# Depthwise stage of a four-layer kernel: weights and image cells loaded into partitions 8 to 119 only

## What is computed

```
A_f, B_f, gA_f, gB_f = FFTs of four 7x7 depthwise kernels
gate_A = sigmoid(ifft(gA_f * x_f));  gate_B = sigmoid(ifft(gB_f * x_f))
a_t = ifft(A_f) * gate_A;            b_t = ifft(B_f * x_f) * gate_B
log_z      = -softplus(-a_t);        log_coeffs = -softplus(a_t)
log_values = log_z + log(softplus(b_t) + 1e-6)
h_final    = exp(last of 8 steps of a log-space scan over (log_coeffs, log_values))
return h_final @ W_out + b_out
```

## Time and profile before

| | |
|---|---|
| median of 3 runs | 5486.84 us (5483.71 to 5490.64) |
| the profiled execution, device time | 5499.24 us |
| its span in the trace | 5497.5 us |
| depthwise stage, from its first to its last convolution | 4539 to 5318 us of the span |
| busy, of the whole span | PE 86%, PEld 63%, DVE 64%, ACT 54%, POOL 37% |
| weights of the depthwise stage | 256 DMAs of 512 KB, 8.1 us from issue to landing |
| windows of the depthwise stage | 128 DMAs of 528 KB, 6.1 us from issue to landing |

### The profile page before, as it was taken

The page is one execution under the profiler, slowest core; times in us unless marked ns, Lnnn a source line. Parts: engine busy times, 40 slices in busy tenths (PEclk is TensorE's granted clock), DMA queues, the critical chain, the costliest instruction groups (busy, mean ns, idle before and its releaser), DMA issues. The chain is left out here.

```text
span 5497.5 us, 111057 instructions
## 1 busy us (share of the span) xinstructions
PE 4738.3 (86%) x37534; PEld 3483.8 (63%) x37534; DVE 3512.8 (64%) x10149; ACT 2975.6 (54%) x6431; POOL 2060.1 (37%) x1516
## 2 busy tenths in 40 slices
PE   6999999999999997469999899974666569999982
PEld 5777777777777775146776677721222348988882
DVE  6778888888888786125666566612899513555554
ACT  1888888888888881123333333332555423555552
POOL 1666666666666660022332233301556300222221
PEclk8999999999999999699999999997999759999995
DMA  7222222222222229742221222255888539999982
GB/s 275 71 71 71 70 71 71 71 71 71 71 71 71 71 60 314 291 139 71 68 68 59 91 67 69 66 183 169 246 272 275 180 123 345 328 325 330 333 260 57
DMA packets 844717, 822.69 MB, mean 150 GB/s; under 512 B 65224, under 2 KB 705665, under 8 KB 835329
## 3 DMA queue, kind: packets, MB, share of 16 engines
q1 hardware_dynamic: 834386, 796.65, 46.5%
q10 hardware_dynamic: 6720, 10.76, 0.6%
q0 software_dynamic: 3072, 8.39, 0.4%
HBM read 607.88 MB, written 207.68 MB: 148 GB/s over the span
## 5 line engine op out<-in xcount | busy, mean ns | idle before, releaser
L299 POOL TENSOR_TENSOR at_bias<-at_tri,at_mask 128x1024 f32<-128x1024 f32 x512 | 1205.1, 2377 | 751.2 <-DVE at_neg_max L460 740.2
L409 ACT ACTIVATE at_probs<-at_neg_s,at_neg_max 128x256 f32<-128x256 f32 x2048 | 894.8, 502 | 0.1
L460 DVE CUSTOM_DVE_ANT_0 at_neg_s<-at_p_s,at_bias 128x256 f32<-128x256 f32 x2048 | 744.1, 420 | 47.1 <-PE at_p_s L333 47.1
L344 PE MATMUL at_p_t<-all_ident,at_probs 128*128 128x128 f32 x4096 | 628.6, 276 | 0.3 <-ACT at_probs_t L401 0.2
L1721 PE MATMUL dw_p_conv<-dw_xw,dw_wts 128*128 128x128 f32 x4096 | 512.9, 278 | 114.9 <-DMA dw_wts<-patch_w 58.5
L344 PEld LDWEIGHTS at_p_t<-all_ident,at_probs 128*128 128x128 f32 x4096 | 484.3, 141 | 136.8 <-issue 85.1
L1721 PEld LDWEIGHTS dw_p_conv<-dw_xw,dw_wts 128*128 128x128 f32 x4096 | 484.5, 192 | 131.6 <-issue 129.5
L921 ACT ACTIVATE ml_h<-ml_p,l_b 128x512 f32<-128x512 f32 x384 | 263.9, 687 | 556.3 <-PE ml_p L880 556.3
L1822 POOL TENSOR_TENSOR dw_xr<-dw_xr,all_b_plain 128x512 f32<-128x512 f32 x128 | 188.1, 1469 | 880.2 <-DMA dw_xr<-x3t 880.2
L468 DVE COPY at_probs_t<-at_p_t 128x512 f32<-128x512 f32 x512 | 352.6, 689 | 205.0 <-PE at_p_t L344 205.0
L889 PE MATMUL ml_p<-l_w1s,ml_h 128*128 128x128 f32 x4096 | 478.4, 275 | 0.8 <-issue 0.8
(11 more groups left out here) (210 smaller groups left out, 9353.4 us busy)
## 6 DMA issues: line engine op xcount, KB each, us to landing
dw_wts<-patch_w SPq DMA_DIRECT2D x256, 512.0 KB, 8.1
dw_xw<-planes SPq DMA_DIRECT2D x128, 528.0 KB, 6.1
sp_xs<-x SPq DMA_DIRECT2D x128, 512.0 KB, 9.9
planes<-pw_plane SPq DMA_DIRECT2D x128, 264.0 KB, 4.5
in_xs<-in_x_dram SPq DMA_DIRECT2D x32, 1024.0 KB, 7.7
at_xs<-in_x_dram SPq DMA_DIRECT2D x256, 128.0 KB, 2.4
at_kvs<-in_L_conv_kv_x_dram SPq DMA_DIRECT2D x256, 128.0 KB, 2.5
at_mask<-in_L_conv_mask_bias_dram SPq DMA_DIRECT2D x256, 128.0 KB, 3.3
```

The lines of the kernel that those rows point to most:

```text
L299: pool.tensor_tensor(bias[:, n % 2, part], tri[:, part], mask[:, n % 4].unsqueeze(1).broadcast_to((128, 4, COLS)), ALU.add).then_inc(maske ...
L344: mm = pe.transpose(p_t[h % 2][:, kh, qh * 128:(qh + 1) * 128], probs[:, h, qh, kh * 128:(kh + 1) * 128], ident[:, :])
L409: e = act.activation(probs[:, h, qh, :], neg_s[:, n % 2, h, qh, :], ACT.Exp, bias=neg_max[:, n % 2, i:i + 1], scale=-1.0)
L460: t = dve.tensor_tensor_reduce(neg_s[:, n % 2, h, qh, :], p_s[h][:, qh, :], bias[:, n % 2, i, :], -1.0, 3.0e38, ALU.add, ALU.min, neg_max[ ...
```

## The change

In the depthwise stage the first filling of each buffer (window loads 0 to 2, weight loads 0 to 3) stays as it is. Every later window load and weight load covers only partitions 8 to 119, 112 of the 128, and reads only those rows from HBM. Partitions 0 to 7 and 120 to 127 keep what the first filling put there: finite image values, and in the weights the zeros of the unused band rows. The number of instructions, their order, the waits and the semaphore counts are as before on every engine; the matmuls still read all 128 partitions.

```diff
-        def windows(b, c):
-
-            at = b * BLOCK_PY * PATCH * PATCH * cell + c * WIDE
-            return bass.AP(planes.tensor, at, [[cell, 128], [PATCH * PATCH * cell, BLOCK_PY], [1, run]])
+        used = slice(PATCH, 128 - PATCH)
+
+        def windows(b, c, first, count):
+
+            at = b * BLOCK_PY * PATCH * PATCH * cell + c * WIDE + first * cell
+            return bass.AP(planes.tensor, at, [[cell, count], [PATCH * PATCH * cell, BLOCK_PY], [1, run]])
...
-                sp.dma_start(flat[:, k % 3], windows(b, c)).then_inc(x_loaded[k % 3], 16)
+                rows = slice(0, 128) if k < 3 else used
+                sp.dma_start(flat[rows, k % 3], windows(b, c, rows.start, rows.stop - rows.start)).then_inc(x_loaded[k % 3], 16)
...
-                sp.dma_start(wts[:, g % 4], patch_w[g % groups]).then_inc(w_loaded[g % 4], 16)
+                rows = slice(0, 128) if g < 4 else used
+                sp.dma_start(wts[rows, g % 4], patch_w[g % groups, rows]).then_inc(w_loaded[g % 4], 16)
```

## The result

| | |
|---|---|
| before | 5488.74 us, median of 4 (5483.71 to 5494.23) |
| after | 5589.16 us, median of 4 (5583.39 to 5605.37) |
| ratio | 1.0188, 95% interval 1.0164 to 1.0211 |
| forecast | 5596 us, 5430 to 5700 us; faster 0.20, the same 0.08, slower 0.72 |

The change reads 25 MB less and costs 100 us. In the profiled executions the span grew from 5497.5 to 5581.7 us, 84 us, and the stage holds all of it: from the first to the last convolution it took 4539.3 to 5317.7 us, and now takes 4537.6 to 5401.4 us, 85 us more.

The account below looks back on a forecast made before the run. The depthwise stage was taken as bound by its loads, and they by the DMA engines. With packets 1.4 times longer, 122 units at +0.89 us gave +109 us on the 5487 us median: 5596 us, range 5430 to 5700 us.

Parts of the forecast that it names:

- What bounds the stage: Depthwise stage: bound by its loads, and they by the DMA engines; PE loses 0.76 us in each 6.44 us unit.
- PE's 5.68 us: Depthwise stage: time PE needs for a unit of 32 convolution matmuls before the loads fall behind.
- the rival in which bytes win: Window and weight loads: rows left cost today's price, m = 1, -61 us, 5426 us; chance 0.20.
- Break-even at m = 1.143: Window and weight loads: m, the factor by which their packets get longer, cancels the saved rows at 8/7.
- 2.64 us for the rest: Main part: engine time a unit that residual loads and stores take, out of 6.87 us.
- The neighbours: Existing loads taken to bound m: kw_sel below at 1.07, residual loads into 32 partitions above at 2.1.
- the 26.6 ns: Price of a 512 B packet where it goes to 128 partitions.
- kw_sel: Load of 49 partitions, lower neighbour for m: 1.07, with about half of the engines at work.
- The sum: Depthwise stage: 122 units, 17 in the first part and 105 later, at 0.89 us each, +109 us.
- 1.067: Main part: overlap factor of DMA records, 6.87 us of engine time passing in 6.44 us.
- m as a property of a load: Window and weight loads: m lengthens the packets of these changed loads; 1.4 taken.
- Signs named in advance: Profile after: DMA share about 1.07 or above, 262 GB/s, 7.33 us units, about 10 first-part units, PE waits 1.6 us.

Follow-up runs that it names:

- the kernel on rows 32 to 95: Kernel with the change, but later window and weight loads cover partitions 32 to 95 instead of 8 to 119, part of the convolution left out: 5479.7 us.
- when it issued 7: Kernel on rows 32 to 95 with residual loads and stores of two units going out together, 7 DMAs a unit from SP instead of 11: 5407.7 us.
- The runs on one half each: Kernel before with only weight loads cut to partitions 8 to 119: 5680.0 us, ratio 1.0342; with only window loads cut: 5649.32 us, ratio 1.0263.
- rows 0 to 63: Kernel with the change, but later window and weight loads cover partitions 0 to 63, part of the convolution left out: 5479.5 us.

## Why the prediction was right, and where its steps were off

- **What bounds the stage**: right in that the loads hold it before and after, with the DMA engines full. It missed the second bound right behind them: SP. The prediction took PE's 5.68 us as the next floor, but SP, issuing 11 DMAs a unit, held the kernel on rows 32 to 95 at 6.3 us, and 5.68 us came only when it issued 7. So the rival in which bytes win was priced too high. That run loaded half of the bytes at uncrowded packet times and gained 19 us against the kernel before beside it; -61 us from an eighth of the bytes was hardly to be had.
- **Break-even at m = 1.143**: the right question. In the first part m measured 1.45 to 1.50. In the main part engine time is 1.10 x 7.16 = 7.88 us a unit, less 2.64 us for the rest, 5.24 us or m = 1.42; the packet times alone (63.5 and 249 ns against 49.2 and 172.9 in the first part before) give 1.39. The forecast was 1.4, between 1.07 and 2.1. It was a choice between neighbours far apart, and neither had the right size, so its closeness is in part luck.
- **The neighbours**: the residual loads pointed the right way but were read too high. In the stretch from 4642 to 4664 us the prediction gave their 2048 packets of 512 B 68 ns each, by subtraction. The trace's records have a mean of 45.9 ns, 1.7 times the 26.6 ns and not 2.6 times; most of the remainder lay on the window packets beside them (74 ns, 49 ns without residual loads). Nor does the place of these loads alone make them slow: the very same residual loads, beside 64-row loads at rows 32 to 95, had 27.5 ns in that stretch. kw_sel, although its form is nearer, was the poorer one; that it met little because half of the engines were idle was not tested.
- **The sum**: by the starts of their convolutions the first sixteen units took 82.9 us instead of 69.6, +0.83 each instead of +0.89. The next eight, without residual loads for the most part, took 43.8 us both times, unchanged as forecast. The other 104 units took 72 us more, +0.69 each instead of +0.89. There 7.88 us of engine time pass in 7.16 us, so the records overlap by a factor of 1.10 and not 1.067; at 1.067 the unit would have been 7.39 us, near the 7.33 forecast. Forecast +109 us; median +100 us, profiled spans +84 us. (A slip without effect: half of the way from 1.4 to 2.1 is m = 1.75, not 1.7.)
- **m as a property of a load**: wrong as worded. The prediction applied m to the packets of the changed loads. The runs on one half each show that whole loads in flight beside them are slowed alike. With both kinds changed the sum comes out the same, so the total did not show it.
- **Signs named in advance**: GB/s 269 (forecast 262), unit 7.16 us (7.33), first part 9.56 units (10), PE's waits 1.2 us a unit by the view (1.6).

## What to carry to other kernels

Count a DMA by the engines and places it uses, not by its bytes: a load of 112 of 128 partitions can be slower than the whole, and it slows the whole loads queued beside it. Where rows are cut, measure the packet times of the set that is left (rows 32 to 95 kept them, rows 0 to 63 doubled them); cutting bytes within all 128 partitions was not tried here. And before a gain is priced down to the next engine's floor, add up what the issuing queue needs for each unit; it does not stand in the busy shares.

## What the runs showed of the hardware

- A 4096 B packet into SBUF took 159 ns with all 128 partitions or partitions 32 to 95 as destination, 332 ns with partitions 0 to 63, 246 ns with 8 to 119 (medians, first part of the stage); 1056 B packets 47, 47, 95 and 72 ns.
- Crowding spreads to others: with the weights in 112 partitions, window packets into all 128 took 75 ns instead of 47; with the windows in 112, whole weight packets took 221 ns instead of 159.
- The same residual loads (512 B packets, four DMAs of 32 partitions each) took 45.9 ns a packet beside whole tiles and 27.5 ns beside loads into partitions 32 to 95 (means, 4642 to 4664 us).
- The same bytes, with residual loads and stores of two units paired into DMAs of twice the size, took 7.45 us of engine time a unit instead of 6.87; the cause is open.
- SP needed 0.43 us (median) to issue a 64 KB store over 32 partitions and 0.60 us over 128. In the run on rows 32 to 95, 11 issues took 5.92 us and held the unit at 6.3 us; with 7 issues it was 5.68 us.
- Residual loads issued by POOL ran as 4096 B packets, those issued by SP as 512 B packets, for the same pieces of 512 B.
